# Attention with scores from two fp32r parts instead of three bf16 parts, heads split over two halves of the array's rows

## What is computed

```python
xn = _layernorm(x, axis=-1)
q, k, v = split_heads(xn @ W_q), split_heads(xn @ W_k), split_heads(xn @ W_v)
q, k = _apply_rope(q, cos, sin), _apply_rope(k, cos, sin)
scores = jnp.einsum('bhqd,bhkd->bhqk', q, k)
scores = jnp.where(causal, -jnp.inf, scores)
attn = jax.nn.softmax(scores / jnp.sqrt(jnp.float32(hd)), axis=-1)
s = merge_heads(jnp.einsum('bhqk,bhkd->bhqd', attn, v)) @ W_o
g = _silu(_L0_ffn_ref(xn, w_router, w_fc, w_proj))
x = x + s * g
```

## Time and profile before

| what | value |
|---|---|
| median of three runs | 2890.48 us |
| profiled execution, its time | 2887.61 us |
| profiled execution, its span | 2885.9 us |
| mean granted TensorE clock | 0.972 |
| TensorE busy over the span | 2595.2 us (90%) |
| VectorE | 2143.5 us (74%) |
| ScalarE | 1749.0 us (61%) |
| POOL | 1011.7 us (35%) |

### The profile page before, as it was taken

How to read it: one execution, slowest core, us unless ns; L and a number is a source line. 1 busy time by engine, 2 the same in 40 slices (tenths; PEclk the granted TensorE clock), 3 DMA queues, 4 the chain that set the end, 5 groups by cost and what they waited for, 6 DMA issues and landing times. The chain is left out here.

```text
span 2885.9 us, 53267 instructions
## 1 busy us (share of the span) xinstructions
PE 2595.2 (90%) x16877; PEld 1267.6 (44%) x16877; DVE 2143.5 (74%) x6184; ACT 1749.0 (61%) x4187; POOL 1011.7 (35%) x1192
## 2 busy tenths in 40 slices
PE   7999967999999999999999999999999997886487
PEld 6888752333333333333333333333333333665366
DVE  7888886888888888888888888888888883342234
ACT  6777742666666666666666666666666665443111
POOL 7888862222222222222222222222222222332663
PEclk9999986999999999999999999999999999998799
DMA  8999977454454554554545545545445422898598
GB/s 280 353 347 355 344 278 132 90 109 84 93 110 86 103 97 82 106 102 88 108 86 94 108 87 98 103 82 108 100 87 111 84 58 82 278 284 292 154 344 304
DMA packets 330056, 453.91 MB, mean 157 GB/s; under 512 B 102960, under 2 KB 242480, under 8 KB 329776
## 3 DMA queue, kind: packets, MB, share of 16 engines
q1 hardware_dynamic: 311728, 398.05, 53.8%
q0 software_dynamic: 18048, 52.45, 7.5%
HBM read 260.06 MB, written 190.84 MB: 156 GB/s over the span
## 5 line engine op out<-in xcount | busy, mean ns | idle before, releaser
L885 DVE CUSTOM_DVE_ANT_0 dump<-ps_rows,mask 128x512 bf16<-128x512 f32 (+7 forms) x2048 | 1482.3, 754 | 349.8 <-issue 253.7
L864 ACT ACTIVATE probs<-ps_cols 128x512 f32<-128x512 f32 (+3 forms) x3072 | 1289.0, 503 | 681.3 <-PE ps_cols L1033 680.7
L1033 PE MATMUL ps_cols<-q_st,k_st 99*128 99x512 bf16 (+3 forms) x3072 | 899.0, 330 | 35.6 <-ACT probs L864 7.4
L977 PE MATMUL ps_rows<-k_st,q_st 96*128 96x512 bf16 (+3 forms) x3072 | 829.6, 330 | 49.9 <-DVE row_max L885 26.4
L843 POOL TENSOR_SCALAR_AFFINE_SELECT probs<-probs 128x512 f32<-128x512 f32 x512 | 324.6, 634 | 1499.1 <-ACT probs L864 1499.1
L1009 PE MATMUL ps_ctx<-probs,v_st 128*32 128x512 f32 (+3 forms) x6144 | 654.6, 498 | 0.6 <-POOL probs L843 0.6
L1033 PEld LDWEIGHTS ps_cols<-q_st,k_st 99*128 99x128 bf16 x3072 | 271.6, 97 | 784.1 <-ACT probs L864 462.6
L977 PEld LDWEIGHTS ps_rows<-k_st,q_st 96*128 96x128 bf16 x3072 | 291.0, 98 | 258.9 <-DVE row_max L885 88.1
L1009 PEld LDWEIGHTS ps_ctx<-probs,v_st 128*32 128x32 f32 x6144 | 120.9, 107 | 182.6 <-issue 91.4
L273 POOL TENSOR_TENSOR roped<-rope_c,rope_s 128x512 f32<-128x512 f32 x128 | 164.8, 1287 | 40.6 <-DVE rope_s L397 40.6
L885 DVE DVE_READ_ACCUMULATOR2_ANT row_max<- 128x1 f32 x2048 | 167.8, 82 | 0.2
(11 more groups left out here) (119 smaller groups left out, 2760.1 us busy)
## 6 DMA issues: line engine op xcount, KB each, us to landing
parts_dram<-parts SPq DMA_DIRECT2D x128, 384.0 KB, 3.8
q_st<-parts_dram SPq DMA_DIRECT2D x384, 128.0 KB
k_st<-parts_dram SPq DMA_DIRECT2D x384, 128.0 KB
v_dram<-v_sb SPq DMA_DIRECT2D x128, 256.0 KB, 5.4
v_st<-v_dram SPq DMA_DIRECT2D x64, 512.0 KB
xs_dram<-zeros SPq DMA_DIRECT2D x36, 512.0 KB, 6.9
xs_sb<-xs_dram SPq DMA_DIRECT2D x72, 256.0 KB
g_dram<-g_sb SPq DMA_DIRECT2D x72, 256.0 KB
```

The costliest lines, as they stand in the source:

```text
L864: nc.scalar.activation(probs[:, k % PB, h, 0:w], ps_cols[(GH * k + h) % CB][:, 0:w], ACT.Exp).then_inc(exp_done, 1)
L885: nc.vector.tensor_tensor_reduce(out=dump[:, even, 0:n], in0=ps_rows[:, 512 * bank:512 * bank + n], in1=mask[:, S - n:S], scale=1.0, scala ...
L977: mm = nc.tensor.matmul(ps_rows[:, 512 * (bank + c):512 * (bank + c) + w], q, k_st[r][0:KS, c, h * 512:h * 512 + w], start=True, stop=True)
L1033: nc.tensor.matmul(ps_cols[(GH * k + h) % CB][:, 0:w], k_st[r][:, j // IB, h * 512 + (j % IB) * P:h * 512 + (j % IB + 1) * P], q_st[r][:, ...
```

## The change

- q and k are cut into two fp32r parts (a rounding by ScalarE, the rest by VectorE). ScalarE's second part, POOL's third part and the buffer between them go. The parts are stored as fp32, 2 x 4 bytes instead of 3 x 2.
- Slots are (0,0,1) against (0,1,0): 48 rows, 50 with the two parts of the maximum. Heads 0 and 1 of a group stand on partitions 0 to 49, heads 2 and 3 on 64 to 113, and the matmuls name that row of the array (`tile_position`). Column matmuls take the heads in the order 0, 2, 1, 3, row items in 2, 0, 3, 1.
- The loads of q and k are 12 DMAs a group as before, 3 slots x 2 halves of the array x 2 tensors. The maxima go in two DMAs instead of one. Their split takes two operations instead of four, and its transpose is fp32.
- The ones that the maxima meet are set by filling all of k_st before the first loads, which wait for that.

```diff
-PARTS = 3
-SLOT_Q = (0, 0, 0, 1, 1, 2)
-SLOT_K = (0, 1, 2, 0, 1, 0)
+PARTS = 2
+SLOT_Q = (0, 0, 1)
+SLOT_K = (0, 1, 0)
+PAIRS = GH // 2
+HALF_ROWS = P // PAIRS
...
-    parts = sb("parts", [P, 2, 4, PARTS, TOK], BF16)
+    parts = sb("parts", [P, 2, 4, PARTS, TOK], F32R)
...
-        def part3(n):
-            pool.wait_ge(part2_done, n + 1)
-            nc.gpsimd.tensor_tensor(parts[:, t % 2, :, 2, s * P:(s + 1) * P],
...
-        def part2(n):
-            act.wait_ge(rest_ready, n + 1)
-            nc.scalar.activation(parts[:, t % 2, :, 1, s * P:(s + 1) * P],
...
-        def take_rest(n):
+        def part2(n):
             dve.wait_ge(part1_done, n + 1)
-            if n >= RR:
-                dve.wait_ge(part3_done, n - RR + 1)
-            nc.vector.tensor_tensor(rest[:, n % RR].rearrange("p (b t) -> p b t", b=4),
+            nc.vector.tensor_tensor(parts[:, t % 2, :, 1, s * P:(s + 1) * P],
                                     ps_m[n % 2][:].rearrange("p (b t) -> p b t", b=4),
-                                    parts[:, t % 2, :, 0, s * P:(s + 1) * P], ALU.subtract).then_inc(rest_ready, 1)
+                                    parts[:, t % 2, :, 0, s * P:(s + 1) * P].bitcast(F32),
+                                    ALU.subtract).then_inc(part2_done, 1)
...
-    q_st = [sb(f"q_st{r}", [KM, HALVES, GH * 512], BF16) for r in range(RING)]
-    k_st = [sb(f"k_st{r}", [KM, HALVES, GH * 512], BF16) for r in range(RING)]
+    q_st = [sb(f"q_st{r}", [P, HALVES, 2 * 512]) for r in range(RING)]
+    k_st = [sb(f"k_st{r}", [P, HALVES, 2 * 512]) for r in range(RING)]
...
+    COL_HEADS = (0, 2, 1, 3)
+    ROW_HEADS = (2, 0, 3, 1)
...
-    MAX_OPS = 4
+    MAX_OPS = 2
...
-            sp.dma_start(q_st[r][KS:KM, c, :], max_T[:, c, :]).then_inc(max_loaded[c], 16)
+            for v in range(PAIRS):
+                sp.dma_start(q_st[r][HALF_ROWS * v + KS:HALF_ROWS * v + KM, c, :],
+                             max_T[2 * IB * PARTS * v:2 * IB * PARTS * (v + 1), c, :]).then_inc(max_loaded[c], 16)
...
         for r in range(RING - 1):
+            sp.wait_ge(ones_set, r + 1)
             load(0, r)
...
+        for r in range(RING):
+            nc.gpsimd.memset(k_st[r][:], 1.0).then_inc(ones_set, 1)
...
                 mm = nc.tensor.matmul(ps_rows[:, 512 * (bank + c):512 * (bank + c) + w], q,
-                                      k_st[r][0:KS, c, h * 512:h * 512 + w], start=True, stop=True)
+                                      k_st[r][head_rows(h, KS), c, at:at + w].bitcast(F32R), start=True, stop=True,
+                                      tile_position=(HALF_ROWS * (h // 2), 0))
...
-                        k_st[r][:, j // IB, h * 512 + (j % IB) * P:h * 512 + (j % IB + 1) * P],
-                        q_st[r][:, c, h * 512 + q0 - 512 * c:(h + 1) * 512],
-                        start=True, stop=True).then_inc(cols_ready, 1)
+                        k_st[r][rows, j // IB, at + (j % IB) * P:at + (j % IB + 1) * P].bitcast(F32R),
+                        q_st[r][rows, c, at + q0 - 512 * c:at + 512].bitcast(F32R),
+                        start=True, stop=True, tile_position=(rows.start, 0)).then_inc(cols_ready, 1)
...
-    parts_dram = nc.dram_tensor("parts_dram", (NT, 4, PARTS, P, TOK), BF16, kind="Internal").ap()
+    parts_dram = nc.dram_tensor("parts_dram", (NT, 4, PARTS, P, TOK), F32, kind="Internal").ap()
```

More of the change, by code:

```diff
@@ L92, in project_phase @@
     roped = sb("roped", [P, RR, 512])
-    rest = sb("rest", [P, RR, 512])
     v_sb = sb("v_sb", [P, 2, NG, SUB, GH * VW])
-    parts = sb("parts", [P, 2, 4, PARTS, TOK], BF16)
+    parts = sb("parts", [P, 2, 4, PARTS, TOK], F32R)
     zeros = sb("zeros", [P, 4 * D])
@@ L257, in _ @@
                        allow_small_or_imprecise_dtypes=True).then_inc(consts_ready, 1)
-        def part3(n):
+        for n in range(NS):
             t, s = divmod(n, SUB)
-            pool.wait_ge(part2_done, n + 1)
-            nc.gpsimd.tensor_tensor(parts[:, t % 2, :, 2, s * P:(s + 1) * P],
-                                    rest[:, n % RR].rearrange("p (b t) -> p b t", b=4),
-                                    parts[:, t % 2, :, 1, s * P:(s + 1) * P],
-                                    ALU.subtract).then_inc(part3_done, 1)
-        for n in range(NS + LAG + 1):
-            t, s = divmod(n, SUB)
-            if n < NS:
-                pool.wait_ge(qk_used, n + 1)
-                if n >= RR:
-                    pool.wait_ge(qkT_ready, n - RR + 1)
-                nc.gpsimd.tensor_tensor(roped[:, n % RR, :], rope_c[:, n % 2, :], rope_s[:, n % 2, :],
-                                        ALU.add).then_inc(roped_ready, 1)
-                if s == SUB - 1 and t + 2 < NT:
-                    rstd_of(t + 2)
-            if n > LAG:
-                part3(n - LAG - 1)
+            pool.wait_ge(qk_used, n + 1)
+            if n >= RR:
+                pool.wait_ge(qkT_ready, n - RR + 1)
+            nc.gpsimd.tensor_tensor(roped[:, n % RR, :], rope_c[:, n % 2, :], rope_s[:, n % 2, :],
+                                    ALU.add).then_inc(roped_ready, 1)
+            if s == SUB - 1 and t + 2 < NT:
+                rstd_of(t + 2)
     @block.scalar
@@ L311, in part1 @@
                                  ps_m[n % 2][:].rearrange("p (b t) -> p b t", b=4), ACT.Copy).then_inc(part1_done, 1)
-        def part2(n):
-            t, s = divmod(n, SUB)
-            act.wait_ge(rest_ready, n + 1)
-            nc.scalar.activation(parts[:, t % 2, :, 1, s * P:(s + 1) * P],
-                                 rest[:, n % RR].rearrange("p (b t) -> p b t", b=4),
-                                 ACT.Copy).then_inc(part2_done, 1)
-        for n in range(NS + LAG + 1):
+        for n in range(NS + LAG):
             t, s = divmod(n, SUB)
@@ L642, in attention_phase @@
     N_DIAG = NB
-    ITEMS = [(i, h) for c in range(HALVES) for i in range(IB * (c + 1) - 1, IB * c - 1, -1) for h in range(GH)]
+    COL_HEADS = (0, 2, 1, 3)
+    ROW_HEADS = (2, 0, 3, 1)
+    ITEMS = [(i, h) for c in range(HALVES) for i in range(IB * (c + 1) - 1, IB * c - 1, -1) for h in ROW_HEADS]
     NI = len(ITEMS)
-    MAX_OPS = 4
+    MAX_OPS = 2
     MAX1_STEP, CTX1_STEP, CTX0_STEP, MAX0_STEP = 1, 1, 7, 7
@@ L893, in split_max @@
             mp = max_parts[:, c]
+            rm = row_max[:, c].rearrange("p (v n) -> p v n", v=PAIRS)
             if i == 0:
@@ L972, in row_item @@
             banks_free(slot, distance)
-            q = q_st[r][0:KS, i // IB, h * 512 + (i % IB) * P:h * 512 + (i % IB + 1) * P]
+            at = h % 2 * 512
+            q = q_st[r][head_rows(h, KS), i // IB, at + (i % IB) * P:at + (i % IB + 1) * P].bitcast(F32R)
             n = (i + 1) * P
```

70 lines of the change are left out of this document (29 added, 41 removed).

## The result

The changed kernel takes **2973.6 us** (median of four runs, 2968.3 to 2977.6) against 2889.3 (2887.3 to 2890.5): a ratio of 1.029, 95% interval 1.027 to 1.031. It is 84 us slower, where 75 us faster was forecast. The profiled execution took 2971.6 us, its span is 2969.9. These are lines of its page. PEclk is the granted clock in tenths of full speed, over 40 equal slices of the span. The lines that start with a line number are groups of instructions: busy us, mean ns of one | idle time before them, and what ended it.

A forecast was written before the change was run, and what follows sets the result against it. It took attention groups (30.5 us) to be bound by chains of waits between engines, VectorE's the longest, not by TensorE streaming. Terms -126 + 13 + 35 + 4 = -74 gave 2815 us; forecast range 2700 to 2885, chance 0.60.

The forecast's parts named there:

- 9 x 0.08 = 0.7 us: Attention group: fp32r weight loads can't hide behind values, giving back up to 0.08 us at about nine VectorE waits.
- VectorE's chain: Attention group: VectorE's work less the shorter split, plus remaining idle time, 28.5 us; the longer chain, taken as the group.
- ScalarE's chain: Attention group: exponentials and score matmuls waiting on each other, 26.7 us plus 12 x 0.08, 27.7 us; below VectorE's chain.
- 9 x 0.22 = 2.0 us: Attention group: about nine times, the first row matmul behind values no longer waits 0.22 us for the column matmul.
- -126 us: Attention stage: groups fall from 30.5 to 28.5 us, -2.0 x 63; bounds -239 to 0.
- upper bound: Attention group up to 30.6 us: 0.09 at both waits of 12 steps, and 1.7 of 3.8 us for row items stays.
- Rival (a): Attention: overlap works but is eaten by latencies, group 29.7 to 30.6 us, total 2892 to 2948, say 2920; chance 0.18.
- Rival (b): Every score matmul: no overlap between halves, +2.2 us a group, +191 us in all, 3080 us; chance 0.16.
- Rival (c), the clock: TensorE's clock falls to 0.50 in the steady attention stretch, over +500 us from values alone; chance 0.03.
- Maxima, +13: Attention: two DMAs for the maxima instead of one arrive late, 0.2 us x 63 groups; bounds 0 and 57.
- Projection, +35: Projection stage: 16.8 MB more stored while DMA engines never rest, +1.09 us x 32 tiles; bounds 0 and 48.
- Start and end, +4: Attention's ends: setting k_st +1.9, second maxima DMA 0.9, last group 1; +4 us.

The follow-up runs named there:

- run 5: Changed kernel with zero-filled rows: row items name 62 rows of their half, column matmuls 64; 2913.1 us, ratio 1.007.
- run 11: Kernel before with the maxima cut into two bf16 parts instead of three, two split operations instead of four; 2793.5 us, ratio 0.982.
- run 14: Two-part bf16 kernel with filled rows, every score matmul naming the whole array instead of one half, so no overlap; ratio 0.981.
- run 13: Changed fp32r kernel with filled rows, every score matmul naming the whole array instead of one half, so no overlap; ratio 1.036.
- run 6: Changed kernel with two bf16 parts instead of fp32r and zero-filled rows, 62 and 64 of each half; 2748.8 us, ratio 0.951.
- run 3: Kernel before with four slots of two bf16 parts instead of six of three, 64 and 67 rows, no halves; 4102 us against 2844.
- Run 7: Changed kernel with each store of parts cut into two DMAs, giving pieces of 1 KB instead of 2 KB; 2985.9 us, ratio 1.033.
- 1: Changed kernel with heads in the old order 0, 1, 2, 3 for column matmuls and row items; 3278 us (3174 and 3383) against 2844.
- 8: Changed kernel with two bf16 parts instead of fp32r and heads in the old order 0, 1, 2, 3; 2989.0 us, ratio 1.035.
- 4: Changed kernel with the first 512 columns of row items i = 4 and 5 computed twice; 3007.3 us, ratio 1.058.
- 2: Changed kernel with q and k in two bf16 parts instead of two fp32r parts, rows not filled; 2757.5 us, ratio 0.970.
- 9: Two-part bf16 kernel with filled rows, heads in the old order 0, 1, 2, 3; ratio 0.968.
- 10: Changed fp32r kernel with filled rows, heads in the old order 0, 1, 2, 3; ratio 1.028.
- 12: Two-part bf16 kernel with filled rows, plus one extra 8-column matmul ahead of each step's first and fourth column matmul; ratio 0.962.
- Run 16: Two-part bf16 kernel with filled rows, plus three extra 8-column matmuls ahead of each step's first column matmul alone; 2851.3 us beside 2889.4.
- run 15: Two-part bf16 kernel with filled rows, plus three extra 8-column matmuls ahead of each step's first and fourth column matmul; 2913.5 us beside 2889.4.

## Why the prediction was wrong

The group at full clock, taken apart by the runs (us; run 5 has the changed kernel's group, 30.52):

| | bf16 | fp32r |
|---|---|---|
| three parts, split of four operations (before) | 30.54 | |
| shorter split (run 11); whole array, two parts (run 14, run 13) | 29.68 | 32.13 |
| halves with overlap (run 6; changed kernel) | 28.39 | 30.53 |

- **The start of the sum was right.** Group of 30.5 us; the split -0.86 (forecast -0.75); the overlap works, and it is worth 1.29 in bf16 and 1.60 in fp32r. That is far less than the 12,928 columns that it takes off the line (5.6 us at 0.43 ns): "not the streaming, since chains rule" held.
- **The step that failed is the price of fp32r behind the waits.** The sum for the forecast had 9 x 0.08 = 0.7 us behind values, against VectorE's chain alone. For ScalarE's chain it had 12 x 0.08, of which nothing counted, since the longer of the two chains was taken, and it had nothing for the fourth column matmul's wait. The runs show that the two chains aren't side by side: the delay stands in TensorE's list, at both waits of a step, and lengthens ten of the twelve steps by some 0.2 us each. fp32r costs 2.14 us a group with overlap, some 1.1 of it behind values and 1.2 behind the exponential's wait. Without overlap it costs 2.45; there TensorE is busy 99% of the time, so the slower pace of fp32r columns counts too.
- **A second term was too large.** The overlap was put at 9 x 0.22 = 2.0 us and gave 1.29 in bf16. So the 2.0 us between the forecast's 28.5 and the measured 30.53 are 1.4 for fp32r and 0.7 for the overlap, less 0.1 for the split. The -126 us became -0.01 x 63, nothing. The forecast's own upper bound said 30.6. Its 0.09 at both waits of 12 steps is near the 0.11 measured; that it also fits in length is partly luck, since its 1.7 us for row items was a choice and it had nothing for the shorter split.
- **Rival (a)** named the mechanism (overlap eaten by latencies) and the length, at 0.18. Its time of 2920 lacked only the clock and had 52 us for DMAs that weren't needed.
- **Rival (b)**: there was overlap. Its price for fp32r, 0.9 + 0.8 + 1.0 = 2.7, was near the 2.45 measured, its group of 32.7 near 32.13.
- **Rival (c), the clock, was given 0.03 and came**, smaller than priced: 63 us in the stage and some 22 at its ends, the whole difference of attention. The evidence against it was the last group, 80% busy at 1.00. But its matmuls had 99 rows. The argument took busy time for what decides; in run 3 TensorE is 100% busy at 0.60. The last group of the changed kernel, with the same work on 50 rows, is mostly at 0.50.
- **Maxima, +13.** SP takes 1.50 us for both DMAs, not 1.8, and between 504 and 2398 us TensorE never waits for them. The term was nothing.
- **Projection, +35.** The sign was wrong. The stage is 5.9 us shorter; the DMA engines moved 398 GB/s where 350 at a share of 0.99 looked like their limit. Run 7 gives the larger pieces 7.5 us, and the bf16 kernels, with 313 GB/s, end the stage only 1.0 us earlier. So time per byte was the wrong price for this stage. What made it 5.9 us shorter than before isn't taken apart: the larger pieces, or the less loaded POOL (151 us busy instead of 253) and ScalarE. The check named in the prediction (attention starting near 465) showed this at once: 423.85.
- **Start and end, +4**: they are where the clock cost 22.

The parts of the difference add up: 2889 - 5.9 + 63 + 22 + 4.5 (experts and output) = 2973.

**What stays open.** The stage's clock, ordered by what the score matmuls name:

| run | rows, place | clock, 504 to 2398 us |
|---|---|---|
| 3 | 64 and 67, whole array | 0.60 |
| 1, 8 | 48 and 50, halves, less overlap | 0.82, 0.88 |
| 4 | 48 and 50, halves, more of the 48 | 0.93 |
| changed, 2 | 48 and 50, halves | 0.96, 0.95 |
| 9, 10 | 62 and 64, halves, less overlap | 0.98, 0.99 |
| 5, 6, 12 | 62 and 64, halves | 0.99 |
| before, 11, 13, 14 | 96 to 128, whole array | 1.00 |

More rows at work at once hold the clock, by filling or by overlap. That filling does is shown cleanly by runs 5 and 6, which change little else; the order of heads changes the overlap and the clock together. What the chip measures isn't shown. Run 16 and run 15 (0.97 at 62 and 64 rows, with 8-column matmuls and waits added) say that it isn't rows alone.

## What to carry to other kernels

Price a weight load at every place where TensorE's list stands still, in both chains at once. A type that loads in 190 instead of 97 ns took the whole gain of the overlap and of the shorter split here, 2.1 us of a 30.5 us group. The same layout in two bf16 parts with filled rows was 5% faster than before, at less precise scores. When matmuls get fewer rows, look at the granted clock first, and fill the rows with zeros: the group at full clock stayed as long, and 60 us came back. Before calling a stage bound by its DMA engines because their share is 0.99, look how busy its other engines are: here TensorE had 95 to 97%. 16.8 MB more than before didn't make the stage longer, and the 33.5 MB less of the bf16 parts made it 1.0 us shorter.

## What the hardware showed that was not expected

- Busy for 1893.78 of 1894 us with 64-row matmuls, TensorE was granted 0.60; with 96 rows at 96% busy, 1.00. Even 30.70 us at full clock, all of them busy, were followed by 297 us at 0.50. Zeros in 14 rows of a half cut the low time from 146.8 to 23.9 us.
- Overlap is won or lost by the order of halves, and the clock with it: the same kernel in another order of heads went from 0.96 to 0.82, and from 1.03 to 1.12 times the time before (3174 to 2844 us) at best.
- The record of a load isn't what it costs: a second bf16 load of 94 ns put the next matmul off by 0.04 us, and fp32r's load, 93 ns longer, by 0.11 where it couldn't go ahead.
- A DMA share of 0.99 at 350 GB/s left room for 398 GB/s, and 313 GB/s in the same stage saved 1.0 us.
